# Four conditioned layers on one core: batch loops written out, one of eight scalings on GpSimd, v projected for two head pairs at once

## The chip, the core and the metric

The kernel runs on one core of one Trainium2 chip. The core has TensorE (matmuls, written PE in the profile, with its weight loads as PEld), VectorE (DVE), ScalarE (ACT), GpSimd (POOL) and SyncE (SP, which issues most DMAs). The metric is the device time of one execution in microseconds (us). Before the change it is 7090.01 us, the median of three runs (7084.36 to 7090.83).

## The reference

x is 8 x 512 x 256 in float32, and goes through four layers, each with a scale and shift from a condition vector:

- layers 0 and 2: attention with 16 heads of 16, then an MLP of 1024 ("narrow"; layer 2 has a padding mask and gates)
- layer 1: attention with 16 heads of 64, so q, k and v have 1024 columns each ("wide"), then an MLP
- layer 3: a selective state space layer (mamba) over the sequence in both directions, then a gated MLP

The parts that matter here, cut to the core:

```python
# layer 1
qkv = x @ W_qkv                      # 256 -> 3 * 1024
q, k, v = jnp.split(qkv, 3, axis=-1) # 16 heads of 64
attn = softmax(einsum('bqhd,bkhd->bhqk', q, k) * scale)
out = einsum('bhqk,bkhd->bqhd', attn, v)
...
# layer 3, one step of the scan, 512 channels (d) with 32 states (n) each
dA = jnp.exp(dt_t[:, :, None] * A)
hst = hst * dA + dt_t[:, :, None] * B_t[:, None, :] * x_t[:, :, None]
y = jnp.einsum('bdn,bn->bd', hst, C_t)
```

## The kernel before

x stays in SBUF for the whole kernel (`x_sb`). Each layer loads its weights, prepares the first batch row, and then runs a loop over the 8 batch rows: `with nc.Fori(0, B) as b` in the narrow layers (L659, used twice), the wide layer (L1082) and the mamba layer (L1723). Such a loop is one body of instructions with a branch back at its end and b in a register. An iteration is a block in which each engine has its own list of instructions, and semaphores order them between engines. It ends in a barrier of all engines, which also clears the semaphores; then come the loop's register operation and its compare-and-branch. The order on each engine is the order in which the Python code issues the instructions.

**Wide layer.** The 16 heads are 8 pairs; q, k and v of a pair fill 128 columns. `project(pair, which, to)` (L991) makes one of them, 512 columns of PSUM wide: for v it runs over 4 tiles of 128 tokens and 2 halves of the depth, with 128 columns of Wv moving, so 8 matmuls (16 records in the profile, since a float32 matmul leaves two). `projected` (L1004) copies the bank to SBUF on ScalarE. An iteration has 32 units (pair, tile of queries). Each has scores, maximum, exponential, a division on GpSimd (`normalise`, L1037), transposes, and the values of the pair before. Query, key and value of a pair (m = 0, 1, 2, ...) are projected in its first three units, two pairs ahead. TensorE heads the iteration, with the scores of a unit.

**Mamba layer.** 512 channels with 32 states are cut into 128 units per batch row: direction w, group g of two states, channel chunk c of 128, with c running fastest, so four units (IC = 4) share a group. For each unit:

- ScalarE makes `decay` = exp(dt * A) in two operations (`decay_unit`, L1803), three buffers deep
- ScalarE scales `dtx_T` (dt * x, tokens on partitions) by a column of B into `dtx_B` (`scale_pair`, L1791): 8 operations (OPS = 4 token tiles x 2 states) for a group of four units, two per unit, made six units ahead
- TensorE turns `dtx_B` around into PSUM (`fill_bx`, L1827) for unit i+1; ahead of a group's first unit it waits for all 8 scalings
- VectorE runs the scan over 2 x 512 elements (`scan_unit`, L1760)
- GpSimd multiplies the states by C, `hc` (L1751), four buffers deep
- TensorE adds `hc` up over the states in PSUM (`y_sum`, L1840), two units behind

At the start of the second direction VectorE also adds the first direction's sum to y, once behind each of four scans (`combine_first`, L1769). After the scans of a batch row comes a stretch called between, which ends this row (gate, output projection, MLP) and prepares the next.

Of the kernel before, what the change touches and what calls it, by code (L numbers as in the profile page):

```python
# [12 lines left out]
FP32 = mybir.dt.float32  # L13
# [7 lines left out]
P = 128  # L21
# [20 lines left out]
NJ = 2  # L42
# [312 lines left out]
def narrow_attention_layer(nc, consts, io, tag, mod0, eps, masked):  # L355
# [27 lines left out]
    with ExitStack() as ctx:  # L383
# [275 lines left out]
        with nc.Fori(0, B) as b:  # L659
# [258 lines left out]
def wide_attention_layer(nc, consts, io, tag, mod0, eps):  # L918
# [21 lines left out]
    with ExitStack() as ctx:  # L940
# [11 lines left out]
        v = sb("v", [P, RING, TT, P], FP32)  # L952
# [38 lines left out]
        def project(pair, which, to):  # L991
            cols = slice(pair * P, (pair + 1) * P)
            if which < 2:
                w = (wq, wk)[which]
                for c in range(DC):
                    last = nc.tensor.matmul(to, w[:, c, cols], hT[:, c, :], start=(c == 0), stop=(c == DC - 1))
            else:
                for t in range(TT):
                    for c in range(DC):
                        last = nc.tensor.matmul(to[:, t * P:(t + 1) * P], hT[:, c, t * P:(t + 1) * P], wv[:, c, cols],  # L1000
                                                start=(c == 0), stop=(c == DC - 1))
            last.then_inc(S["proj_filled"], 1)

        def projected(pair, which, of):  # L1004
# [4 lines left out]
            elif which == 1:  # L1009
                nc.scalar.activation(kT[:, pair % RING, :], of, ACT.Copy).then_inc(S["proj"], 1)  # L1010
            else:
                nc.scalar.activation(v[:, pair % RING, :, :].rearrange("p t n -> p (t n)"), of, ACT.Copy)\
                    .then_inc(S["proj"], 1)
# [68 lines left out]
        with nc.Fori(0, B) as b:  # L1082
# [4 lines left out]
            with nc.Block() as block:  # L1087
# [100 lines left out]
                def _(pe):  # L1188
# [11 lines left out]
                    def values(pair, k):  # L1200

                        if k == 0:
                            for j in range(2):
                                pe.wait_ge(S[f"probs_T{j}"], TT * (pair + 1))
                            if pair >= LEAD_PAIRS:
                                pe.wait_ge(S["proj"], 3 * (pair - LEAD_PAIRS + 1))
                            if pair:
                                pe.wait_ge(S["oT"], pair)
                        for j in range(2):
                            last = nc.tensor.matmul(bank[PV][head(j), :], v[:, pair % RING, k, head(j)],  # L1210
# [118 lines left out]
def mamba_layer(nc, consts, io, tag, mod0, eps):  # L1329
# [27 lines left out]
    with ExitStack() as ctx:  # L1357
        def sb(name, shape, dt, where=ctx):
# [23 lines left out]
            "y_init", "dtx", "dtxT_filled", "dtxT", "dt_rep", "zero", "c_rep", "dtxB", "decay", "bx_filled", "scan",  # L1382
# [340 lines left out]
        with nc.Fori(0, B) as b:  # L1723
            nxt = (b + 1) % B
            x_of_b = x[:, bass.ds(b, 1), :, :].rearrange("p b t d -> p (b t) d")
            with nc.Block() as block:
# [15 lines left out]
                def _(pool):  # L1742
                    nc.gpsimd.memset(decay[:, :, :, 0:1], 0.0).then_inc(S["zero"], 1)
                    for i in range(UNITS):
                        if i % IC == 0:
# [44 lines left out]
                def _(act):  # L1790
                    def scale_pair(q):  # L1791
# [5 lines left out]
                        for op in (2 * c, 2 * c + 1):  # L1797
# [28 lines left out]
                def _(pe):  # L1826
                    def fill_bx(i):  # L1827
                        k, c = i // IC, i % IC
                        if c == 0:
                            pe.wait_ge(S["dtxB"], OPS * (k + 1))  # L1830
# [136 lines left out]
```

## Time and profile before

| what | us |
|---|---|
| runs, median of 3 | 7090.01 (7084.36 to 7090.83) |
| the profiled execution | 7084.28 |
| its span, first to last instruction | 7082.4 |
| layer 0, with what comes first (12 to 1098) | 1086 |
| wide layer's loop (1098 to 2678) | 1580, TensorE busy 1509.27 |
| layer 2 (2678 to 3796) | 1118 |
| mamba layer's loop (3796 to 7068) | 3272, ScalarE busy 2881.24, VectorE 2771.48, TensorE 2698.68, GpSimd 2076.94 |
| busy over the span | PE 86%, PEld 45%, DVE 67%, ACT 64%, POOL 35% |

Times in the profile are microseconds from the start of the span, unless marked ns. A row of a timeline has start, length, engine, line, operation, out<-in and how many were merged (x4); in brackets stands how long the engine sat idle before it, and what ended that: "<-ACT l__decay L1808" is ScalarE's instruction of line 1808, a q behind an engine is its sequencer (waits, branches, barriers), and "issue" means that it waited for nothing that the profile shows. A row of a group has count, busy time, mean ns of one, and the idle time ahead of its instructions. Records of ScalarE overlap by about a tenth, so the pace of one is read from starts or counts, not from its length. The granted clock of TensorE (PEclk) is 1.00 at 2.4 GHz and 0.50 at 1.2 GHz; over the span it is 0.940.

### The profile page before, as it was taken

The page shows a single profiled execution, that of the slowest core. Times are in us where ns is not written, and L with a number is a line of the kernel's source. Part 1 is how long each engine was busy: PE and PEld are TensorE (multiplying, and loading weights), DVE is VectorE, ACT ScalarE, POOL GpSimd, SP SyncE. Part 2 cuts the span into 40 slices and gives each one's busy share as a digit, 9 for nine tenths or more (in the row PEclk, how much of TensorE's full clock was granted, in tenths as well). Part 3 has the DMA queues.
Part 4 walks back from the last instruction along what each step waited for, and adds up shares of the span by engine and source line. Part 5 has one row for each costly group of instructions (what it writes and reads, how often), then busy time and mean ns, then how long its engine had stood idle before and what let it go on. Part 6 is the DMA issues. An engine that isn't in the chain of part 4 may idle for free. (4 is left out here: it accounts for less than half of the span.)

```text
span 7082.4 us, 80931 instructions
## 1 busy us (share of the span) xinstructions
PE 6066.9 (86%) x29464; PEld 3179.4 (45%) x29464; DVE 4715.9 (67%) x5217; ACT 4502.5 (64%) x7301; POOL 2499.3 (35%) x1718
## 2 busy tenths in 40 slices
PE   6998988999999996898977878878888888888887
PEld 3544444555555553444443444444444444444444
DVE  4666654433433445666666979889797979979797
ACT  2343434544444452443437979798897979889796
POOL 0000002222222220000004838477483847658383
PEclk8999999999999997999998989999898989989898
DMA  3313140000000002313131010110101010010102
GB/s 104 54 27 54 27 83 8 1 1 1 1 1 1 1 1 51 57 29 57 29 72 43 28 38 27 27 37 20 46 27 37 28 36 29 19 48 26 39 27 56
DMA packets 162612, 229.57 MB, mean 32 GB/s; under 512 B 24784, under 2 KB 97816, under 8 KB 161776
## 3 DMA queue, kind: packets, MB, share of 16 engines
q1 hardware_dynamic: 162144, 225.09, 14.2%
q8 instruction: 215, 3.52, 0.2%
q14 instruction: 109, 0.89, 0.0%
q10 hardware_dynamic: 144, 0.07, 0.0%
HBM read 153.06 MB, written 33.72 MB: 26 GB/s over the span
## 5 line engine op out<-in xcount | busy, mean ns | idle before, releaser
L1766 DVE TENSOR_TENSOR_SCAN l__h<-l__decay,l__psum 128x1024 f32<-128x1024 f32 x1024 | 2331.9, 2284 | 208.2 <-ACT l__decay L1808 145.0
L1751 POOL TENSOR_TENSOR l__hc<-l__h,l__c_rep 128x1024 f32<-128x1024 f32 x1024 | 2050.5, 2002 | 545.1 <-DVE l__h L1766 509.3
L1835 PE MATMUL l__psum<-ident,l__dtx_B 128*128 128x128 f32 x8192 | 1141.4, 284 | 494.4 <-ACT l__dtx_B L1799 475.7
L1835 PEld LDWEIGHTS l__psum<-ident,l__dtx_B 128*128 128x128 f32 x8192 | 898.1, 143 | 1328.9 <-ACT l__dtx_B L1799 698.9
L1799 ACT ACTIVATE l__dtx_B<-l__dtx_T,l__b_T 128x512 f32<-128x512 f32 x2048 | 1353.2, 711 | 0.1
L1808 ACT ACTIVATE l__decay<-l__dt_rep,l__a_neg 128x511 f32<-128x511 f32 x2048 | 1351.5, 711 | 0.0
L1846 PE MATMUL l__psum<-l__hc,l__gather 128*64 128x512 f32 x4096 | 1108.6, 620 | 17.1 <-POOL l__hc L1751 17.1
L107 POOL TENSOR_SCALAR l__ln_var_eps<-l__ln_mean_var 128x4 f32<-128x4 f32 x70 | 16.0, 229 | 2447.6 <-DVE l__ln_mean_var L93 2447.6
L566 DVE TENSOR_REDUCE l__row_max<-l__psum 128x1 f32<-128x512 f32 x1072 | 688.4, 686 | 257.3 <-PE l__psum L581 255.8
L1039 POOL TENSOR_SCALAR l__probs<-l__probs,l__rec 128x512 f32<-128x512 f32 x516 | 352.4, 696 | 1013.0 <-DVE l__rec L1035 1013.0
L752 ACT ACTIVATE l__probs<-l__psum 128x1024 f32<-128x1024 f32 x512 | 515.6, 1025 | 272.4 <-PE l__psum L799 267.9
L1025 DVE TENSOR_REDUCE l__neg_max<-l__psum 128x2 f32<-128x1024 f32 x258 | 315.2, 1222 | 472.3 <-PE l__psum L1019 472.3
L581 PE MATMUL l__psum<-l__k_stack,l__q_stack 96*128 96x512 bf16 (+1 forms) x1072 | 435.1, 418 | 143.1 <-PEq L915 92.8
L1160 ACT ACTIVATE l__probs_T<-l__psum 128x512 f32<-128x512 f32 x256 | 152.8, 597 | 471.0 <-PE l__psum L1196 471.0
L1030 ACT ACTIVATE l__probs<-l__psum,l__neg_max 128x512 f32<-128x512 f32 x516 | 349.4, 683 | 47.3 <-DVE l__neg_max L1025 30.1
L1019 PE MATMUL l__psum<-l__kT,l__qT 64*128 64x512 f32 x1032 | 298.6, 656 | 62.7 <-issue 50.3
L799 PE MATMUL l__psum<-l__q_stack,l__k_stack 98*128 98x512 bf16 (+1 forms) x1024 | 330.3, 413 | 8.7 <-ACT l__probs L752 4.4
L1196 PEld LDWEIGHTS l__psum<-ident,l__probs 128*128 128x128 f32 x2048 | 224.8, 143 | 203.6 <-POOL l__probs L1039 121.7
L581 PEld LDWEIGHTS l__psum<-l__k_stack,l__q_stack 96*128 96x128 bf16 (+1 forms) x1072 | 103.2, 98 | 443.0 <-DVE l__row_max L566 294.0
L902 PE MATMUL l__psum<-l__w,l__g 128*128 128x256 f32 x1024 | 285.6, 380 | 12.4 <-ACT l__g L772 12.4
L1846 PEld LDWEIGHTS l__psum<-l__hc,l__gather 128*64 128x64 f32 x4096 | 203.8, 135 | 204.5 <-issue 130.0
L1196 PE MATMUL l__psum<-ident,l__probs 128*128 128x128 f32 x2048 | 288.6, 284 | 0.7
(168 smaller groups left out, 7112.9 us busy)
## 6 DMA issues: line engine op xcount, KB each, us to landing
l__c_rep<-l__c_dram SPq DMA_DIRECT2D x512, 128.0 KB, 2.8
l__dt_rep<-l__dt SPq DMA_DIRECT2D x144, 256.0 KB, 5.0
l__parts_dram<-l__parts SPq DMA_DIRECT2D x72, 384.0 KB, 4.5
l__q_stack<-l__parts_dram SPq DMA_DIRECT2D x216, 128.0 KB, 6.8
l__k_stack<-l__parts_dram SPq DMA_DIRECT2D x216, 128.0 KB, 9.8
l__w<-in_l_w SPq DMA_DIRECT2D x6, 1024.0 KB, 9.0
mod_w<-in_mod_w SPq DMA_DIRECT2D x2, 2816.0 KB, 12.6
x_sb<-in_x SPq DMA_DIRECT2D x1, 4096.0 KB, 27.3
```

The source lines that it names most:

```text
L566: nc.vector.tensor_reduce(mx[:, h // GH, t, h % GH:h % GH + 1], max_bank(n), AX.X, ALU.max).then_inc(S["max_taken"], 1)
L581: nc.tensor.matmul(max_bank(n), qs[0:k_max, h, t * P:(t + 1) * P], ks[0:k_max, h, :], start=True, stop=True).then_inc(S["max_filled"], 1)
L752: nc.scalar.activation(probs[:, n % SLOTS:n % SLOTS + 2, :], pair(n), ACT.Exp, scale=float(HD) ** -0.5).then_inc(S["exp"], 1)
L1030: nc.scalar.activation(probs[:, u % SLOTS, j, :], bank[QK + 2 * (u % 2) + j], ACT.Exp, bias=neg_max[:, u % SLOTS, j:j + 1], accum_out=sums ...
L1039: nc.gpsimd.tensor_scalar(probs[:, u % SLOTS, j, :], probs[:, u % SLOTS, j, :], rec[:, u % SLOTS, j:j + 1], 1.0, ALU.mult, ALU.mult)\
L1196: last = nc.tensor.transpose(bank[TR + j][:, k * P:(k + 1) * P], probs[:, u % SLOTS, j, k * P:(k + 1) * P], ident[:, :])
L1751: nc.gpsimd.tensor_tensor(hc[:, i % HCS, :, :], h[:, i % HS, :, :], c_of_i, ALU.mult).then_inc(S["hc"], 1)
L1766: nc.vector.tensor_tensor_scan(both(h[:, i % HS, :, :]), both(decay[:, i % DECAYS, :, :]), both(bx_psum(i)), 0.0, ALU.mult, ALU.add).then_ ...
L1799: nc.scalar.activation(dtx_B[:, k % 2, t, :, j, :], dtx_T[:, w, t, :].rearrange("p (b d) -> p b d", d=HB), ACT.Copy, scale=b_T[:, w, t, NJ ...
L1808: nc.scalar.activation(decay[:, i % DECAYS, s, 1:T], dt_rep[:, w, c, s, 1:T], ACT.Exp, scale=a_neg[:, g, c, s:s + 1]).then_inc(S["decay"], 1)
L1835: last = nc.tensor.transpose(bx_psum(i)[:, s, t * P:(t + 1) * P], dtx_B[:, k % 2, t, 2 * c + s, :, :].rearrange("p j d -> p (j d)"), ident ...
L1846: last = nc.tensor.matmul(y_psum[half(s), c, :], gather[:, :], hc[:, i % HCS, s, :], start=(g == 0), stop=(g == GROUPS - 1))
```

## The change

Three edits.

1. All three `nc.Fori` become Python loops: the body stands in the program eight times, b is a number, and there is no branch back. The barrier and the clearing of semaphores stay.
2. In the mamba layer the last of a group's 8 scalings (tile 3, state 1) goes from ScalarE to GpSimd, as a tensor_scalar with its own semaphore, `dtxB_pool`. GpSimd makes it one group ahead. TensorE's wait ahead of a group is now for 7 scalings of ScalarE per group and one of GpSimd.
3. In the wide layer a v projection covers 256 columns (two pairs) and two of the four token tiles; the two projections of two neighbouring pairs together make what they made before. The buffer of v is laid out for this: 2 slots of double width in place of 4. Values of an even pair wait for both.

```diff
-        with nc.Fori(0, B) as b:
+        for b in range(B):
...
-        v = sb("v", [P, RING, TT, P], FP32)
+        v = sb("v", [P, RING // 2, TT, 2 * P], FP32)
...
             else:
-                for t in range(TT):
+                both = slice(pair // 2 * 2 * P, (pair // 2 + 1) * 2 * P)
+                for u in range(2):
+                    t = pair % 2 * 2 + u
                     for c in range(DC):
-                        last = nc.tensor.matmul(to[:, t * P:(t + 1) * P], hT[:, c, t * P:(t + 1) * P], wv[:, c, cols],
-                                                start=(c == 0), stop=(c == DC - 1))
+                        last = nc.tensor.matmul(to[:, u * 2 * P:(u + 1) * 2 * P], hT[:, c, t * P:(t + 1) * P],
+                                                wv[:, c, both], start=(c == 0), stop=(c == DC - 1))
...
-                                pe.wait_ge(S["proj"], 3 * (pair - LEAD_PAIRS + 1))
+                                pe.wait_ge(S["proj"], 3 * (pair // 2 * 2 + 2 - LEAD_PAIRS))
...
                     nc.gpsimd.memset(decay[:, :, :, 0:1], 0.0).then_inc(S["zero"], 1)
+
+                    def scale_last(k):
+                        w, g, _ = split(k * IC)
+                        t, j = TT - 1, NJ - 1
+                        if k >= 2:
+                            pool.wait_ge(S["bx_filled"], IC * (k - 1))
+                        nc.gpsimd.tensor_scalar(dtx_B[:, k % 2, t, :, j, :],
+                                                dtx_T[:, w, t, :].rearrange("p (b d) -> p b d", d=HB),
+                                                b_T[:, w, t, NJ * g + j:NJ * g + j + 1], 1.0,
+                                                ALU.mult, ALU.mult).then_inc(S["dtxB_pool"], 1)
+
+                    scale_last(0)
                     for i in range(UNITS):
+                        if i % IC == 0 and i // IC + 1 < UNITS // IC:
+                            scale_last(i // IC + 1)
...
-                        for op in (2 * c, 2 * c + 1):
+                        for op in (2 * c, 2 * c + 1)[0:1 if c == IC - 1 else 2]:
...
-                            pe.wait_ge(S["dtxB"], OPS * (k + 1))
+                            pe.wait_ge(S["dtxB"], (OPS - 1) * (k + 1))
+                            pe.wait_ge(S["dtxB_pool"], k + 1)
```

ScalarE at the start of a batch row of the mamba layer, in the kernel before (L1799 is the scaling, L1808 the decay):

```order
226 L1799 ACT_TABLE_LOAD
227 L1799 ACTIVATE l__dtx_B<-l__dtx_T,l__b_T 128x8x64 x8
228 L1808 ACTIVATE l__decay<-l__dt_rep,l__a_neg 128x511 x4
229 L1799 ACTIVATE l__dtx_B<-l__dtx_T,l__b_T 128x8x64 x4
230 L1808 ACTIVATE l__decay<-l__dt_rep,l__a_neg 128x511 x2
231 L1799 ACTIVATE l__dtx_B<-l__dtx_T,l__b_T 128x8x64 x2
232 L1808 ACTIVATE l__decay<-l__dt_rep,l__a_neg 128x511 x2
233 L1799 ACTIVATE l__dtx_B<-l__dtx_T,l__b_T 128x8x64 x2
```

The same place after the change (L1816 is now the scaling, L1825 the decay):

```order
1251 L1816 ACTIVATE l__dtx_B<-l__dtx_T,l__b_T 128x8x64 x7
1252 L1825 ACT_TABLE_LOAD
1253 L1825 ACTIVATE l__decay<-l__dt_rep,l__a_neg 128x511 x4
1254 L1816 ACTIVATE l__dtx_B<-l__dtx_T,l__b_T 128x8x64 x4
1255 L1825 ACTIVATE l__decay<-l__dt_rep,l__a_neg 128x511 x2
1256 L1816 ACTIVATE l__dtx_B<-l__dtx_T,l__b_T 128x8x64 x2
1257 L1825 ACTIVATE l__decay<-l__dt_rep,l__a_neg 128x511 x2
1258 L1816 ACTIVATE l__dtx_B<-l__dtx_T,l__b_T 128x8x64
```

One scaling of the first eight is gone, and every fourth pair after them is a single one. The load of the function table, which stood ahead of the first scaling, now stands ahead of the first decay; it is one per batch row as before.

GpSimd at the same place, before:

```order
93 L1721 ISA
94 L1723 UNCONDITIONAL_BRANCH
95 L1741 UNCONDITIONAL_BRANCH
96 L1743 MEMSET l__decay 128x6
97 L1751 TENSOR_TENSOR l__hc<-l__h,l__c_rep 128x1024 x128
98 L107 TENSOR_SCALAR l__ln_var_eps<-l__ln_mean_var 128x4
```

And after:

```order
252 L1724 ISA
253 L1744 UNCONDITIONAL_BRANCH
254 L1746 MEMSET l__decay 128x6
255 L1753 TENSOR_SCALAR l__dtx_B<-l__dtx_T,l__b_T 128x8x64 x2
256 L1768 TENSOR_TENSOR l__hc<-l__h,l__c_rep 128x1024 x4
257 L1753 TENSOR_SCALAR l__dtx_B<-l__dtx_T,l__b_T 128x8x64
258 L1768 TENSOR_TENSOR l__hc<-l__h,l__c_rep 128x1024 x4
```

Two scalings now stand ahead of the first product, and one ahead of every fourth.

TensorE at a turn of the wide layer's loop, before (rows 179 and on are the body's head, to which the branch goes back):

```order
303 L1019 MATMUL l__psum<-l__kT,l__qT 128x512 x2
304 L1290 MATMUL l__psum<-l__w,l__g 128x256 x32
305 L1087 UNCONDITIONAL_BRANCH
306 L1082 REGISTER_ALU
307 L1082 COMPARE_AND_BRANCH
```

And the first turn after the change, with the first v projection (L1002):

```order
1315 L1293 MATMUL l__psum<-l__w,l__g 128x256 x32
1316 L1090 UNCONDITIONAL_BRANCH
1317 L1190 UNCONDITIONAL_BRANCH
1318 L1022 MATMUL l__psum<-l__kT,l__qT 128x512 x2
1319 L1199 MATMUL l__psum<-ident,l__probs 128x128 x8
...
1324 L1022 MATMUL l__psum<-l__kT,l__qT 128x512 x2
1325 L1199 MATMUL l__psum<-ident,l__probs 128x128 x8
1326 L1002 MATMUL l__psum<-l__wv,l__hT 128x256 x4
```

The register operation and the branch back are gone, the next row's scores follow at once, and a v projection has 4 matmuls of 256 columns where it had 8 of 128. The rest of the order on TensorE is the same.

## Rows read from the trace of the kernel before

**Rows 1.** Groups of instructions, mamba scans, 6700 to 6965 us; idle before them last:

```profile
L1766 DVE TENSOR_TENSOR_SCAN l__h<-l__decay,l__psum 128x1024 f32<-128x1024 f32 x109 | 248.7, 2285 | 16.3 <-ACT l__decay L1808 16.3
L1751 POOL TENSOR_TENSOR l__hc<-l__h,l__c_rep 128x1024 f32<-128x1024 f32 x109 | 218.2, 2002 | 48.8 <-DVE l__h L1766 48.0 <-PE l__psum L1846 0.8
L1799 ACT ACTIVATE l__dtx_B<-l__dtx_T,l__b_T 128x512 f32<-128x512 f32 x217 | 143.2, 706 | 0.0
L1808 ACT ACTIVATE l__decay<-l__dt_rep,l__a_neg 128x511 f32<-128x511 f32 x217 | 142.9, 705 | 0.0
```

**Rows 2.** Timeline of one group of four units: start, length, engine, line:

```profile
6703.79 2.29 DVE L1766 TENSOR_TENSOR_SCAN l__h<-l__decay,l__psum 128x1024 f32<-128x1024 f32 x1 [0.17 <-ACT l__decay L1808]
...
6706.22 2.00 POOL L1751 TENSOR_TENSOR l__hc<-l__h,l__c_rep 128x1024 f32<-128x1024 f32 x1 [0.45 <-DVE l__h L1766]
6706.24 2.29 DVE L1766 TENSOR_TENSOR_SCAN l__h<-l__decay,l__psum 128x1024 f32<-128x1024 f32 x1 [0.16 <-ACT l__decay L1808]
...
6707.43 1.09 PE L1835 MATMUL l__psum<-ident,l__dtx_B 128*128 128x128 f32 x8 [1.60 <-ACT l__dtx_B L1799]
```

**Rows 3.** Timeline of VectorE, second direction's start and scans at an iteration's end:

```profile
6829.05 2.27 DVE L1766 TENSOR_TENSOR_SCAN l__h<-l__decay,l__psum 128x1024 f32<-128x1024 f32 x1
...
6831.83 2.27 DVE L1766 TENSOR_TENSOR_SCAN l__h<-l__decay,l__psum 128x1024 f32<-128x1024 f32 x1
...
6973.25 8.82 DVE L1766 TENSOR_TENSOR_SCAN l__h<-l__decay,l__psum 128x1024 f32<-128x1024 f32 x4 [0.17 <-ACT l__decay L1808]
```

**Rows 4.** Timeline of GpSimd in the wide layer, a steady unit:

```profile
1309.97 1.36 POOL L1039 TENSOR_SCALAR l__probs<-l__probs,l__rec 128x512 f32<-128x512 f32 x2 [2.44 <-DVE l__rec L1035]
```

**Rows 5.** Timeline of a turn of the wide layer, VectorE's and TensorE's first:

```profile
1292.48 0.17 DVE L1101 COPY l__cur<-mod 128x12 f32 x1 [1.83 <-PEq L1296]
...
1295.95 2.08 PE L1019 MATMUL l__psum<-l__kT,l__qT 64*128 64x512 f32 x4 [7.48 <-issue]
```

**Rows 6.** Timeline of the entry into the wide layer's loop:

```profile
1098.09 2.08 PE L1019 MATMUL l__psum<-l__kT,l__qT 64*128 64x512 f32 x4 [6.12 <-PEq L1080]
1098.23 0.17 DVE L1101 COPY l__cur<-mod 128x12 f32 x1 [2.82 <-PEq L1080]
```

**Rows 7.** Instructions of line 1082: engine, count, ns min/median/max, first and last start:

```profile
L1082 PEldq COMPARE_BRANCH  x8: 79/3507/3849, 1292.0 to 2677.4; - x8
...
L1082 PEldq MOVE  x1: 29/29/29, 1098.0 to 1098.0; - x1
```

**Rows 8.** Timeline of mamba's loop: entry, first turn, last turn; GpSimd and ScalarE:

```profile
3796.40 0.11 POOL L1743 MEMSET l__decay<- 128x6 f32 x1 [78.35 <-POOLq L1721]
3796.41 1.28 ACT L1799 ACT_TABLE_LOAD   x1 [11.15 <-PEq L1721]
...
4203.34 0.11 POOL L1743 MEMSET l__decay<- 128x6 f32 x1 [51.32 <-POOLq L1860]
...
4205.96 1.28 ACT L1799 ACT_TABLE_LOAD   x1 [11.15 <-issue]
...
6658.99 0.11 POOL L1743 MEMSET l__decay<- 128x6 f32 x1 [50.99 <-POOLq L1860]
...
6661.89 1.28 ACT L1799 ACT_TABLE_LOAD   x1 [12.44 <-issue]
```

**Rows 9.** The same as rows 7, for line 659 of the narrow layers:

```profile
L659 PEldq COMPARE_BRANCH  x16: 76/211/242, 241.0 to 3700.9; - x16
```

**Rows 10.** Layer 0's first two rows: us, PE, PEld, DVE, ACT, POOL busy (count), PEclk:

```profile
125.80:241.20 115.40, 105.27 (x496) 52.75 (x496) 71.62 (x128) 49.44 (x59) 2.53 (x4) 0.96 0.26 42
241.20:356.70 115.50, 105.41 (x496) 52.92 (x496) 71.65 (x128) 49.47 (x59) 2.53 (x4) 0.96 0.27 41
```

**Rows 11.** Stretch at the first turn of the wide layer, columns as in rows 10:

```profile
1296.00:1300.60 4.60, 4.60 (x14) 2.58 (x15) 1.86 (x2) 1.49 (x4) 0.00 (x0) 0.50 0.03 7
```

**Rows 12.** Timeline of TensorE: a v projection, and a down projection:

```profile
1323.36 1.95 PE L1000 MATMUL l__psum<-l__wv,l__hT 128*128 128x128 f32 x16
...
1274.39 14.08 PE L1290 MATMUL l__psum<-l__w,l__g 128*128 128x256 f32 x64
```

More of the change, by code:

```diff
@@ L1011, in projected @@
             else:
-                nc.scalar.activation(v[:, pair % RING, :, :].rearrange("p t n -> p (t n)"), of, ACT.Copy)\
+                half = slice(pair % 2 * 2, pair % 2 * 2 + 2)
+                nc.scalar.activation(v[:, pair // 2 % 2, half, :].rearrange("p t n -> p (t n)"), of, ACT.Copy)\
                     .then_inc(S["proj"], 1)
@@ L1080, in wide_attention_layer @@
         nc.all_engine_barrier(sems_to_clear=S.range)
-        with nc.Fori(0, B) as b:
+        for b in range(B):
             nxt = (b + 1) % B
@@ L1209, in values @@
                         for j in range(2):
-                            last = nc.tensor.matmul(bank[PV][head(j), :], v[:, pair % RING, k, head(j)],
+                            last = nc.tensor.matmul(bank[PV][head(j), :], v[:, pair // 2 % 2, k, pair % 2 * P + HD1 * j:pair % 2 * P + HD1 * (j + 1)],
                                                     probs_T[:, pair % 2, j, k, :], start=(k == 0), stop=(k == TT - 1))
@@ L1381, in mamba_layer @@
             "dc_filled", "dc", "bT_filled", "bT", "c_out", "dt_filled", "abs", "exp_abs", "ln", "relu", "dt", "y_first",
-            "y_init", "dtx", "dtxT_filled", "dtxT", "dt_rep", "zero", "c_rep", "dtxB", "decay", "bx_filled", "scan",
+            "y_init", "dtx", "dtxT_filled", "dtxT", "dt_rep", "zero", "c_rep", "dtxB", "dtxB_pool", "decay", "bx_filled", "scan",
             "hc", "y_sum", "combine", "gated", "y_filled", "res", "up_filled", "silu", "prod", "down_filled"])
@@ L1721, in mamba_layer @@
         nc.all_engine_barrier(sems_to_clear=S.range)
-        with nc.Fori(0, B) as b:
+        for b in range(B):
             nxt = (b + 1) % B
```

## The prediction

> **What bounds the kernel now.** I read the page first (shares and the 40 slices in the table above), then the groups of instructions, then the timeline of single units and of the loops' turns, because the change touches three stages with different limits.
>
> The last layer's loop (mamba) takes 3272 of the 7082 us. In its scans the groups of one quiet stretch of 265 us [rows 1] show ScalarE with no idle time before any of its operations (0.0 in both groups, 217 + 217 operations). 265 / 434 gives 0.611 us for one, though each record is 0.71 long, because they overlap. VectorE's scan (2.285) waits 16.3 us there, all of it for ScalarE's decay; GpSimd's 109 products (2.002) wait 48.8 us, 0.45 each, for the scan. In the timeline [rows 2] a scan starts 0.16 us after VectorE came free, for a decay, and 2.45 us after the one before; in these ScalarE does two scalings and two decays, 0.6125 us each. TensorE waits 1.60 us once per group of four units, for the last dtx_B. So ScalarE sets this stage: 4 x 2.45 = 9.80 us per group, 256 groups in the kernel.
>
> What is next behind it? Where decays are ready, four scans take 8.82 us: (8.82 - 2.285) / 3 = 2.18 apart [rows 3]. That is 8.72 us a group. GpSimd has 4 x 2.00 = 8.0. TensorE has 9.80 - 1.60 = 8.2.
>
> In the wide layer TensorE is busy nearly all the time inside an iteration; at its turns it isn't, nor is anything else.
>
> **GpSimd scales one of eight.** ScalarE loses one operation per group, 32 per iteration, 256 in all: 256 x 0.6125 = 156.8 us. All of them lie ahead of the last scaling of an iteration, and only the last four scans are already at VectorE's pace [rows 3], so the whole sum reaches the end if 9.80 - 0.61 = 9.19 us per group can be held by the others:
> - VectorE needs 8.72. The decays now come 2.45, 2.45, 2.45 and 1.84 apart; after the short step a scan is 0.34 late, and the next two steps give it back. Where the second direction begins, a combination stands behind each of four scans, and they come 2.78 apart [rows 3]: 4 x 2.78 - 9.19 = 1.9 late, given back at 0.47 a group. ScalarE stalls only if scans are over 3.2 us late, so that is absorbed: its decays of unit i+2 start 1.4 us ahead of scan i+2, and wait for the end of scan i-1, which is the start of scan i, two scans of 2.3 earlier.
> - TensorE needs 8.2. Its first fill of a group waits for two semaphores; ScalarE's still comes last. That fill and the decay of the same unit end together now; the 0.34 above covers it. Behind the wait stand the y sums and three fills: they have 1.0 us left of the 1.6.
> - GpSimd gets the scaling: a tensor_scalar of 128x512 with a column as factor. The trace has this on GpSimd in the wide layer, two in 1.36 us [rows 4], one each 0.68. Sum 8.0 + 0.7 = 8.7 of 9.19. New is the form (8 pieces of 64, 128 apart in the destination). I bound it by 0.67 below and by the 2.00 of the two-input product above [rows 1], and take 0.68, the row with the same operation, inputs and size. The scaling is made a whole group ahead of its fill. It stands ahead of the product of the group's first unit, which then ends 0.6 us later; the y sum of it is behind a fill that waits for scan 4k+1, so nobody waits. Its wait for the buffer is met before it comes.
>
> **Loops written out: turns.** A turn has a barrier in both kernels; what goes is the branch back. In the wide layer TensorE starts 3.47 us after VectorE's first copy at a turn [rows 5], but 0.14 before it where the loop is entered without a branch [rows 6]. The sequencer's COMPARE_BRANCH lasts 3.51 us in the median against 0.03 for the MOVE at the entry [rows 7]; TensorE's scores head the iteration, so this is on the path: 7 x 3.5 = 24.6 us. In the mamba layer ScalarE heads the iteration. Its first instruction is 2.62 and 2.90 us behind GpSimd's memset at the first and the last turn, but 0.01 at the entry [rows 8]; with about 0.1 for the register work of the branch I take 2.8: 7 x 2.8 = 19.6 us. The table load that stood there now comes after the first seven scalings; there is still one, so the sum stays. In the narrow layers TensorE's branch takes 0.21 [rows 9]: 14 turns x 0.27 = 3.8 us.
>
> The Trainium skill has another price: by "Advanced Engine Details and Errata", section Control Flow Timing, a compare-and-branch costs about 108 ns. By it 28 turns would give 28 x 0.11 = 3 us in place of the 48. The narrow row is near it and the wide one 30 times above, so the rule doesn't hold for the long bodies; it is the third rival below.
>
> Does straight code run slower than a loop already passed? The narrow layer's first iteration runs code that no one has run before, the second repeats it: TensorE's 496 matmuls took 105.27 and 105.41 us in stretches of 115.4 and 115.5 [rows 10]. I cost it at nothing.
>
> TensorE's clock: after the turn it is granted 0.50 (1.2 GHz) for the wide layer's first 4.6 us [rows 11], behind 7.5 us of idle TensorE [rows 5]. With 4 us idle the low stretch may go or fall wholly behind the start: 4.6 us at half the clock costs 2.3, so 7 x 2.3 = 16 us either way. I take 0, as both ends are equally near.
>
> **v for two head pairs.** 66 projections, each 16 records of 128 columns before, (1.95 - 0.28) / 15 = 0.112 apart, and 8 of 256 now; these stand 14.08 / 64 = 0.218 apart in the down projection [rows 12]. 16 x 0.112 = 1.79 against 8 x 0.218 = 1.74: 3 us in all, at least 0 if TensorE waits elsewhere. Values of an even pair now wait for the projection of the next pair, three later; but the projection of query 9 is ahead of them in TensorE's order and had already waited for 9 copies where 6 are asked. No copy is added.
>
> **Sum.** 156.8 + 24.6 + 19.6 + 3.8 + 3.1 = 208 us, against the profiled execution: 7084.3 - 208 = 6876. That execution is at the low end of the three runs; their median is 5.7 above it. I forecast 6878.
>
> **The rivals.**
> - GpSimd becomes the bound. For: it is the closest new load, its form is new, and a product that waits starts 0.14 us after the scan's end [rows 2]. Against: [rows 4]. If the strided scaling takes twice as long, 1.36, and a product 2.05, a group is 9.56 in place of 9.19: 256 x 0.37 = 95 back, 6972. Chance 0.10.
> - The turns stay, since new code has to be brought in for every block. Against it stand the entries, which are also new code. 48 us don't come: 6925. Chance 0.08 (by the skill's rule above: 6877 + 45 = 6922).
> - Slower than before: GpSimd's scaling at 2.0, the row of the product, with each product paying such a wait, 0.15: 4 x 2.15 + 2.0 = 10.6 a group against 9.80, 256 x 0.8 = +205, less 51 of turns and v: 7084 + 154 = 7238. It decides from a group of 10.0 us, a scaling of 1.4 in that case. Chance 0.03.
> - VectorE becomes the bound at 2.18 plus the 0.16 of a wait at each scan [rows 2], 9.36 a group: 256 x 0.17 = 44 back, 6921. Against: such waits only arise when VectorE is early. Chance 0.06.
>
> **Numbers.** The forecast has 0.73. It spans 6850 (clock stretches gone, 16, and the turns at their longest, 10) to 6895. For 8 in 10 I reach to the cases at 6921 and 6925: 6850 to 6930. A change under 0.2% (14 us) can't be told from none here; faster by more 0.94, within 0.02, slower 0.04.
>
> **What would show it.** Right: scans 2.30 us apart in the mean in quiet stretches, ScalarE still with 0.0 idle ahead of dtx_B and decay, 1792 scalings on ScalarE and 256 on GpSimd near 0.7 us, GpSimd's idle ahead of the products down to about 0.1 a unit; no COMPARE_BRANCH at the turns, TensorE starting within 0.3 us of VectorE's first copy. A mamba iteration goes from 409.5 to about 387 us, a wide one from 197.9 to 194. Wrong: ScalarE waiting for scans, TensorE waiting for GpSimd at the first fill of a group, GpSimd without idle time, or gaps called "issue" at new places where code is brought in.

## The result, and the profile after

The changed kernel takes 6866.4 us in the median of 4 runs (6864.8 to 6877.0), the one before 7087.2 on the same chip (4 runs, 7083.2 to 7090.8). The ratio is 0.9692, with a 95% interval of 0.9675 to 0.9709: 3.1% faster. The forecast was 6878, in a range of 6850 to 6930. The profiled execution of after took 6865.4 us, with a span of 6863.6. Both spans, cut where VectorE ends the last addition of each layer:

| stretch | before | after | change | predicted |
|---|---|---|---|---|
| start and layer 0 (narrow) | 1045.9 | 1042.9 | -3.0 | -1.9 |
| wide layer | 1630.2 | 1583.7 | -46.5 | -27.7 |
| layer 2 (narrow) | 1023.5 | 1026.1 | +2.6 | -1.9 |
| mamba layer | 3367.6 | 3195.1 | -172.5 | -176.4 |
| sum | 7067.2 | 6847.8 | -219.4 | -208 |

The saving is 11 us larger than forecast. The wide layer gave 19 us more and layer 0 1; layer 2 and the mamba layer gave 4.5 and 4 less. So the total came nearer than the wide layer's term did, which is partly luck.

The groups of after in a quiet stretch of the mamba layer, 6500 to 6765 us (busy and mean ns, then idle time before), answer to [rows 1]:

```profile
L1783 DVE TENSOR_TENSOR_SCAN l__h<-l__decay,l__psum 128x1024 f32<-128x1024 f32 x115 | 256.0, 2272 | 6.3 <-ACT l__decay L1825 3.8
L1768 POOL TENSOR_TENSOR l__hc<-l__h,l__c_rep 128x1024 f32<-128x1024 f32 x116 | 231.2, 2005 | 17.2 <-DVE l__h L1783 13.3 <-PE l__psum L1864 0.3
L1825 ACT ACTIVATE l__decay<-l__dt_rep,l__a_neg 128x511 f32<-128x511 f32 x228 | 165.6, 846 | 0.3 <-DVE l__h L1783 0.3
L1816 ACT ACTIVATE l__dtx_B<-l__dtx_T,l__b_T 128x512 f32<-128x512 f32 x193 | 144.2, 846 | 0.0
...
L1753 POOL TENSOR_SCALAR l__dtx_B<-l__dtx_T,l__b_T 128x512 f32<-128x512 f32 x27 | 18.9, 699 | 0.0
```

There are 115 scans in 265 us, 2.30 apart where 109 were 2.43 apart by the same count. ScalarE still has no idle time to speak of, and GpSimd's before its products is down from 48.8 to 17.2 us. The scans that begin two neighbouring groups, against [rows 2]:

```profile
6199.38 9.04 DVE L1783 TENSOR_TENSOR_SCAN l__h<-l__decay,l__psum 128x1024 f32<-128x1024 f32 x4 [0.17 <-ACT l__decay L1825]
...
6208.59 4.46 DVE L1783 TENSOR_TENSOR_SCAN l__h<-l__decay,l__psum 128x1024 f32<-128x1024 f32 x2 [0.16 <-ACT l__decay L1825]
```

They are 9.21 us apart. The row merges its four scans, since it leaves out idle time of about 0.1 us. Taken one by one they start at 6199.38, 6201.59, 6203.76 and 6206.14. Two of the four still wait for a decay, 0.17 and 0.11 us, and start 2.45 and 2.38 behind the one before. The two behind ScalarE's single scaling find their decays made and start 2.21 and 2.17 behind, which is VectorE's own pace.

The turns. First the wide layer, VectorE's and TensorE's first instructions and a v projection, against [rows 5] and [rows 12]:

```profile
1286.21 0.17 DVE L1104 COPY l__cur<-mod 128x12 f32<-128x12 f32 x1 [1.25 <-PEq L1299]
1286.21 1.13 PE L1022 MATMUL l__psum<-l__kT,l__qT 64*128 64x512 f32 x4 [3.43 <-PEq L1299]
...
1295.81 1.89 PE L1002 MATMUL l__psum<-l__wv,l__hT 128*128 128x256 f32 x8
```

TensorE starts with VectorE, not 3.47 us behind it. It was idle for 3.43 us instead of 7.48, and the same four score matmuls take 1.13 us, not 2.08: they run at full clock. The v projection's eight records take 1.89 us where sixteen took 1.95. The stretches of 6 us behind the first, fifth and sixth turn show where that holds (length, busy time and count of PE, PEld, DVE, ACT and POOL, then the granted clock, DMA share and GB/s; compare [rows 11]):

```profile
1286.20:1292.20 6.00, 5.99 (x29) 3.25 (x30) 4.08 (x9) 3.08 (x7) 1.51 (x2) 1.00 0.00 0
...
2050.80:2056.80 6.00, 5.67 (x18) 2.85 (x20) 3.38 (x8) 2.12 (x6) 1.50 (x2) 0.72 0.01 3
2243.90:2249.90 6.00, 5.88 (x20) 2.92 (x20) 2.84 (x7) 2.38 (x6) 0.49 (x1) 0.72 0.01 3
```

At five of seven turns the clock stays at 1.00 (2.4 GHz), and the row behind them takes 191.17 us. At the fifth and sixth it is at 0.50 for part of the stretch, and the rows take 193.1 and 192.7. In the kernel before it was at 0.50 behind every turn.

The first turn of the mamba layer, against [rows 8]:

```profile
4135.64 0.11 POOL L1746 MEMSET l__decay<- 128x6 f32 x1 [51.09 <-POOLq L1878]
...
4135.66 4.40 ACT L1816 ACTIVATE l__dtx_B<-l__dtx_T,l__b_T 128x512 f32<-128x512 f32 x7 [8.02 <-PEq L1878]
...
4140.08 1.28 ACT L1825 ACT_TABLE_LOAD   x1
```

ScalarE starts 0.02 us behind GpSimd instead of 2.62; the table load stands behind the seven scalings. A mamba row takes 387.2 to 387.8 us (one 389.0) instead of 409.6 (one 408.3).

### The profile page after: what moved, and what is told of

The parts are those of the page before. It is cut to its first block and busy times, and to the rows that moved or that the text cites. A ratio compares the mean times of both kernels' runs of the same rounds, so it can differ in the third digit from the quotient of the medians.

```text
span 6863.6 us, 79140 instructions
## 1 busy us (share of the span) xinstructions
PE 6055.9 (88%) x28936; PEld 3147.6 (46%) x28936; DVE 4662.2 (68%) x5217; ACT 4353.0 (63%) x7044; POOL 2655.6 (39%) x1974
## 5 line engine op out<-in xcount | busy, mean ns | idle before, releaser
L1783 DVE TENSOR_TENSOR_SCAN l__h<-l__decay,l__psum 128x1024 f32<-128x1024 f32 x1024 | 2279.5, 2273 | 115.5 <-ACT l__decay L1825 92.4
L1825 ACT ACTIVATE l__decay<-l__dt_rep,l__a_neg 128x511 f32<-128x511 f32 x2048 | 1491.2, 850 | 2.4 <-DVE l__h L1783 2.3
L1816 ACT ACTIVATE l__dtx_B<-l__dtx_T,l__b_T 128x512 f32<-128x512 f32 x1792 | 1334.7, 845 | 69.6 <-PEq L1878 59.7
L581 PE MATMUL l__psum<-l__k_stack,l__q_stack 96*128 96x512 bf16 (+1 forms) x1072 | 436.4, 419 | 138.3 <-PEq L915 88.5
```

The lines of the kernel that those rows point to most:

```text
L581: nc.tensor.matmul(max_bank(n), qs[0:k_max, h, t * P:(t + 1) * P], ks[0:k_max, h, :], start=True, stop=True).then_inc(S["max_filled"], 1)
L1783: nc.vector.tensor_tensor_scan(both(h[:, i % HS, :, :]), both(decay[:, i % DECAYS, :, :]), both(bx_psum(i)), 0.0, ALU.mult, ALU.add).then_ ...
L1816: nc.scalar.activation(dtx_B[:, k % 2, t, :, j, :], dtx_T[:, w, t, :].rearrange("p (b d) -> p b d", d=HB), ACT.Copy, scale=b_T[:, w, t, NJ ...
L1825: nc.scalar.activation(decay[:, i % DECAYS, s, 1:T], dt_rep[:, w, c, s, 1:T], ACT.Exp, scale=a_neg[:, g, c, s:s + 1]).then_inc(S["decay"], 1)
```

## The experiments

The parts alone come first, all against runs of before on the same chip (median 7092.3).

**e1, the scaling alone.** The kernel before, with part 2 of the change and none of the others.

```diff
+                    scale_last(0)
...
-                        for op in (2 * c, 2 * c + 1):
+                        for op in (2 * c, 2 * c + 1)[0:1 if c == IC - 1 else 2]:
```

> The kernel before with one of a group's 8 scalings on GpSimd, loops and v as before. Theory (ScalarE sets the stage, 9.80 us per group becomes 9.20): 256 x 0.60 = 154 us less, 6931, and the mamba rows lose 19 us each, the first as the others; turns keep the 2.6 us of ScalarE behind GpSimd. Rival (part of the 172 us that the mamba layer lost comes from straight code or the clock, not from the scaling): under 140 us less, with groups above 9.3 us.

Measured: 6941.0 us, ratio 0.9793 (0.9777 to 0.9810), 151 less. The groups from 5000 to 5080 us:

```profile
L1780 DVE TENSOR_TENSOR_SCAN l__h<-l__decay,l__psum 128x1024 f32<-128x1024 f32 x36 | 80.4, 2274 | 2.3 <-ACT l__decay L1822 1.5
L1765 POOL TENSOR_TENSOR l__hc<-l__h,l__c_rep 128x1024 f32<-128x1024 f32 x36 | 71.7, 2001 | 5.2 <-DVE l__h L1780 4.0
L1822 ACT ACTIVATE l__decay<-l__dt_rep,l__a_neg 128x511 f32<-128x511 f32 x71 | 46.8, 707 | 0.0
L1813 ACT ACTIVATE l__dtx_B<-l__dtx_T,l__b_T 128x512 f32<-128x512 f32 x61 | 40.7, 708 | 0.0
```

ScalarE still never stops. The mamba layer takes 3214.2 us, 153.4 less, with groups of 9.18 to 9.19. This part of the mamba layer's gain doesn't need straight code. Layer 2, untouched here, took 1033.2 us instead of 1023.5; of that below.

**e2, the loops alone.**

```diff
-        with nc.Fori(0, B) as b:
+        for b in range(B):
```

(three times)

> The kernel before with all three loops written out and nothing else. Theory (a branch less at each turn, and TensorE's clock kept at the wide turns): wide turns 7 x (3.5 + 2.5) = 42, mamba turns 7 x 2.6 = 18, narrow layers 3 less in layer 0 and 3 more in layer 2, in all 60 us less, 7024. Rival 1 (the branch alone, as predicted): 48 less, 7036. Rival 2 (branches cost 0.11 us each): 3 less, 7081.

Measured: 7033.3 us, ratio 0.9923 (0.9906 to 0.9939), 59 less. The total is as my theory has it, its parts aren't. Wide rows are 194.5 us, 3.4 below 197.9, and not 191.9: the clock is still at 0.50 behind six of the seven turns, and for part of the stretch at the first (a row of 193.3). Mamba rows are 406.2, 3.4 less instead of 2.6. Layer 0 is 2.5 shorter, layer 2 is 1.2 shorter.

The 3.4 has two parts. TensorE started 4.8 to 5.3 us behind the last addition of the row before; now it starts 1.25 behind it (1.48 at one turn). That is 3.7 us in the mean. But the clock is low for 6.0 us behind that start where it was low for 5.3, which at half the clock takes 0.37 back. Take from each of the seven wide rows TensorE's start and half of the time at 0.50 behind it, and 190.26 to 190.27 us are left in the kernel before, 190.26 to 190.35 here.

**e3, the wide loop alone.** The same edit in the wide layer only.

> The kernel before with the wide layer's loop alone written out. Theory (branch 3.5 us a turn, and the stretch at 1.2 GHz behind it gone, which cost 2.3 to 2.5): wide rows from 197.9 to 191.9 us, some of them 1.7 longer where the clock still falls; 39 to 42 us less in all, 7043. Rival (the branch alone, the low stretch only moves): rows of 194.4, 25 less, 7060; the 46 us that the wide layer lost would then need v for the rest.

Measured: 7062.2 us, ratio 0.9962 (0.9947 to 0.9976), 30 less. Rows: 191.6, 193.6, then five of 194.45 to 194.55. Five are the rival's and one is the theory's: the rows get 3.4 shorter where the clock still falls, and keeping it comes on top only at some turns. In the whole layer 27.6 us are gone.

**e4, v for two pairs alone.**

> The kernel before with v projected for two pairs at once and nothing else. Theory: 66 projections, each 0.05 us shorter: 3 us less, 7081, not to be told from none by the time, but 0.4 us less in each wide row by the trace. Rival (256 columns are worth more in this place, or a wait on values goes): wide rows shorter by 1 to 2.5 us, 8 to 20 us in all, 7066 to 7076, which would explain the wide layer's surplus without the clock.

Measured: 7089.8 us, ratio 0.9997 (0.9987 to 1.0007), no difference by the time. By the trace the wide layer is 4.0 us shorter; with TensorE's start and the low clock taken out as above, all seven rows are 0.46 shorter (189.8 for 190.27). So v doesn't hold the wide layer's surplus by its own work.

**e5, TensorE late and idle.** The changed kernel; at seven turns TensorE first waits for GpSimd.

```diff
+    LATE = 5
...
+                    if b:
+                        for n in range(LATE):
+                            nc.gpsimd.tensor_scalar(g[:, n, :], hT[:, 0, :], 1.0, 1.0, ALU.mult,
+                                                    ALU.mult).then_inc(S["late"], 1)
...
+                    if b:
+                        pe.wait_ge(S["late"], LATE)
```

> The changed kernel, but at 7 turns of the wide layer TensorE waits for five scalings of 128x512 that GpSimd makes first (into a buffer that isn't in use there). Clock theory: TensorE starts 3.4 us later, as after the branch in the kernel before, its clock falls to 0.50 for the first 4 to 5 us, and a wide row gets 3.4 + 2.3 = 5.7 us longer: 35 to 40 us more than the changed kernel, 6903. Rival (the surplus of the wide layer has another cause than TensorE's idle time at the turn): 3.4 us a row, 24 more, 6890, clock at 1.00 behind the turn.

Measured: 6899.1 us, 33 above the changed kernel; the wide layer is 34 us longer. A turn of it in the timeline, and the 6 us behind VectorE's first copy:

```profile
1291.19 2.98 POOL L1097 TENSOR_SCALAR l__g<-l__hT 128x512 f32<-128x512 f32 x5 [12.87 <-SPq L1091]
1294.22 2.08 PE L1023 MATMUL l__psum<-l__kT,l__qT 64*128 64x512 f32 x4 [6.46 <-POOL l__g L1097]
```

```profile
1291.10:1297.10 6.00, 2.88 (x8) 1.38 (x9) 0.93 (x2) 0.00 (x0) 2.98 (x5) 0.50 0.00 0
```

TensorE is 3.0 us late (the five scalings stand 0.6 apart), idle for 6.46, and starts at 1.2 GHz at every turn: rows of 195.6 to 197.1, 4.5 to 5.9 above 191.17. The clock's part is 1.5 to 2.9 us a row. This run alters TensorE's idle time at the turn and none of its work: with 6.46 us in place of 3.43 the clock is at 0.50 at the start of seven rows out of seven, where it was at one.

**e6, TensorE late and busy.** The changed kernel with the first scores' matmuls six times more ahead of them.

```diff
+    MORE = 6
...
+                        for n in range(MORE):
+                            for j in range(2):
+                                nc.tensor.matmul(bank[QK + j], qT[head(j), 0, LEAD * P:(LEAD + 1) * P],
+                                                 kT[head(j), 0, :], start=True, stop=True)
```

> The changed kernel, but at 7 turns of the wide layer TensorE first makes the matmuls of its first scores six times more (the results are overwritten by the same). They take 6 x 0.57 = 3.4 us, the same delay as in the run with the wait. Clock theory: TensorE is busy, so the clock stays at 1.00 where it stood so before; 3.4 us a row, 24 more, 6890. Rival (a late start costs the 2.3 whatever TensorE does): 5.7 a row, 40 more, 6906.

Measured: 6911.3 us. I had mis-sized the matmuls. They appear as one row of the timeline at the first turn, and as one at the third:

```profile
1287.92 5.42 PE L1228 MATMUL l__psum<-l__kT,l__qT 64*128 64x512 f32 x24 [3.43 <-PEq L1305]
```

```profile
1682.23 7.12 PE L1228 MATMUL l__psum<-l__kT,l__qT 64*128 64x512 f32 x24 [3.42 <-PEq L1305]
```

At full clock they cost 5.2 us, and that row is 196.3 long, 5.1 above 191.17: a late start costs only its length if the clock stays. At the other six turns the clock was low for part of them, 1.7 us more, and rows are 198.0. So this run doesn't separate the theories by its total, and the clock theory's "stays at 1.00" did not come true. It shows something else: the idle time at the turn is 3.43 us as in the changed kernel, yet the clock falls at six turns where there it fell at two.

**e13, the idle time at the turn halved.** The loops alone (e2), and two matmuls at the end of a row.

```diff
+                    for n in range(2):
+                        nc.tensor.matmul(bank[TR], w1[:, n, 0:P], hT_mlp[:, n, :], start=(n == 0), stop=(n == 1))
```

> The kernel before with all loops written out, as in the run with the loops alone, and at the end of each wide row TensorE makes two matmuls more into a bank that nothing reads (1.9 us, while VectorE adds the last half of the row, so no later barrier). In the run with the loops alone TensorE's clock was at 0.50 for 5 us behind six of seven wide turns (rows of 194.5 us) and held at none but one (193.3). Theory (the clock falls for the 3.4 us that TensorE is idle at the turn): idle is 1.5 us now, the clock stays at 1.00, wide rows 191.6, 6 x 2.9 + 1.7 = 19 us less than 7033: 7014. Rival (idle time at the turn isn't what lets it fall): rows of 194.5 again, 7033.

Measured: 7016.9 us (7015.7 to 7021.3, 4 runs), ratio 0.9889 (0.9873 to 0.9906), 16 below the loops alone (on another chip). The start of a row in this run:

```profile
1287.67 1.13 PE L1019 MATMUL l__psum<-l__kT,l__qT 64*128 64x512 f32 x4 [1.71 <-PEq L1298]
```

Stretches behind the first three turns here, and then behind the same turns with the loops alone:

```profile
1287.60:1293.60 6.00, 5.93 (x18) 3.15 (x20) 3.38 (x8) 2.28 (x6) 1.50 (x2) 0.72 0.01 3
1480.90:1486.90 6.00, 5.92 (x29) 3.20 (x30) 4.01 (x9) 3.01 (x7) 1.50 (x2) 1.00 0.01 4
1672.60:1678.60 6.00, 6.00 (x29) 3.23 (x30) 4.09 (x9) 3.09 (x7) 1.51 (x2) 1.00 0.00 0
```

```profile
1287.00:1293.00 6.00, 5.93 (x18) 3.12 (x20) 3.38 (x8) 2.29 (x6) 1.51 (x2) 0.72 0.00 0
1480.30:1486.30 6.00, 5.93 (x15) 3.31 (x16) 2.89 (x7) 1.93 (x5) 0.54 (x1) 0.50 0.03 7
1674.90:1680.90 6.00, 5.98 (x15) 3.30 (x16) 2.94 (x7) 1.93 (x5) 0.59 (x1) 0.50 0.00 0
```

In 6 us TensorE makes 29 matmuls instead of 15. Rows are 191.63 at five of seven turns (193.3 and 193.5 at the other two), 2.9 below 194.5, with more work in them. The wide layer is 15.6 us shorter, and the clock's worth is measured: 2.9 us a turn.

The cause isn't shown by this run alone. The first turn has the same partial fall as with the loops alone, and the changed kernel holds the clock at five turns too, with the full 3.43 us of idle time. All traces together say this: behind 6.5 to 7.5 us of idle time the clock was at 0.50 when TensorE started, at 28 turns of 28 (before, e1, e4, e5); behind 3.4 to 3.7 us it fell at 33 turns of 63 (e2, e3, e6 to e10, e12 and the changed kernel); behind 1.7 to 1.9 us, at 2 of 7. So the long idle time brings the fall, which e5 shows by itself; at 3.4 us and below, idle time alone doesn't settle it.

**e12, the changed kernel again.** No edit.

> The changed kernel once more, unaltered, for its profile and time on the chip of these runs. Theory (whether TensorE's clock falls at a wide turn is not settled by the program; two kernels with the same wide layer had rows of 191.15 throughout and rows of 191.2 to 194.2): the wide rows again are 191.2 where the clock holds and 192.7 to 194.5 where it falls, but not in the same rows as in the first profile; mamba groups again 9.20. Rival (the program settles it): the same rows as in the first profile, 193.1 and 192.7 at the sixth and seventh.

Measured: 6869.4 us (6860.0 to 6871.6, 5 runs), ratio 0.9686 (0.9673 to 0.9699). The theory fell: wide rows are 191.17 with 193.08 and 192.71 at the sixth and seventh, as in the first profile, to 0.03 us. The pattern comes back in the same program. It isn't settled by the wide layer's own code, which is the same in e7, e8 and e10 below: there the clock falls behind none of the seven turns, five, and three. Mamba groups are 9.19.

**e10, narrow loops kept.** The changed kernel with `nc.Fori` in layers 0 and 2.

> The changed kernel with the loop of the narrow layers (0 and 2) kept as a loop. Theory (the branch costs 0.27 us a turn there, and the changed kernel's longer rows in layer 2 are the clock's, not the straight code's): layer 0 gets 2 to 3 us longer, layer 2 the same but for its clock, 3 to 4 us in all, under what the time can tell. Rival (straight code costs layer 2 time): layer 2 loses no rows of 120.1 us and the kernel is 3 to 6 us faster.

Measured: 6881.5 us (6859.1 to 6882.8, 5 runs), ratio 0.9696 (0.9680 to 0.9712), which overlaps that of e12 in the same comparison. The trace: the last seven rows of layer 0 take 806.3 us as in the kernel before, against 803.0 in the changed one, 3.3 for seven turns. Layer 2 takes 1035.1 us, not less than 1026.1: straight code isn't what made it longer. The wide layer is 6 us longer: 4 in its seven rows, through the clock at the first three turns, and 2 ahead of the end of its first row. The prediction has no term for what stands behind the end of a loop. Up to the end of the first row the wide layer takes 243.1 to 244.8 us in the five traces with narrow loops (before, e1, e3, e4, e10), 242.0 to 242.7 in the others.

Now the next bound behind ScalarE.

**e7, the scaling made twice.** The changed kernel; after GpSimd's scaling the same again, with a wait for the first.

```diff
+                        pool.wait_ge(S["dtxB_pool"], 2 * k + 1)
+                        nc.gpsimd.tensor_scalar(dtx_B[:, k % 2, t, :, j, :],
...
```

> The changed kernel with GpSimd's scaling made twice in a row into the same place. GpSimd then has 4 x 2.005 + 2 x 0.70 = 9.4 us of work per group, ScalarE 9.20 as before. Theory (GpSimd costs the group nothing until its own sum is above ScalarE's): 9.4 to 9.5 per group, 256 x 0.2 to 0.3 = 51 to 77 us more than the changed kernel, 6917 to 6943, with GpSimd without idle time. Rival 1 (GpSimd is already bound up with each scan, so its work adds in full): 256 x 0.70 = 179 more, 7045. Rival 2 (nothing waits for GpSimd within buffers): no change.

Measured: 6896.3 us, ratio 0.9727 (0.9711 to 0.9743), 30 above the changed kernel (the mamba layer of the profiled execution is 19 us longer). Groups are 9.30 us where GpSimd has come to bind, and still 9.19 in about the first ten of a row. In a stretch of eight groups (5126.30 to 5200.74 us) its products have no idle time before them, and VectorE now waits for them:

```profile
L1788 DVE TENSOR_TENSOR_SCAN l__h<-l__decay,l__psum 128x1024 f32<-128x1024 f32 x34 | 75.0, 2267 | 4.4 <-POOL l__hc L1773 3.4 <-ACT l__decay L1830 1.0
L1773 POOL TENSOR_TENSOR l__hc<-l__h,l__c_rep 128x1024 f32<-128x1024 f32 x33 | 65.1, 2003 | 0.0
```

A second scaling of 0.70 costs the group 0.11. The theory has the mechanism right and the size wrong: 30 us instead of 51 to 77, since GpSimd is faster than was taken, as the next run shows.

**e8, two of eight on GpSimd.**

```diff
+        on_pool = lambda k: 2
...
+                        for op in range(OPS - on_pool(k), OPS):
...
+                            if op >= OPS - on_pool(k):
+                                continue
```

> The changed kernel with two of a group's 8 scalings on GpSimd in place of one. ScalarE has 14 x 0.613 = 8.6 us per group, VectorE 8.72, GpSimd 4 x 2.005 + 2 x 0.70 = 9.4. Theory (GpSimd becomes the bound): 9.4 to 9.5 per group, 51 to 77 us more than the changed kernel, 6917 to 6943. Rival (ScalarE still is, or GpSimd runs beside it): 8.7 to 8.8 per group, 100 to 128 less, 6740 to 6766.

Measured: 6872.6 us, ratio 0.9690 (0.9674 to 0.9706), no different from the changed kernel. Neither expectation was right; the groups are 9.19. GpSimd in its timeline:

```profile
5150.89 1.41 POOL L1755 TENSOR_SCALAR l__dtx_B<-l__dtx_T,l__b_T 128x512 f32<-128x512 f32 x2
5152.21 7.92 POOL L1770 TENSOR_TENSOR l__hc<-l__h,l__c_rep 128x1024 f32<-128x1024 f32 x4
5160.07 1.41 POOL L1755 TENSOR_SCALAR l__dtx_B<-l__dtx_T,l__b_T 128x512 f32<-128x512 f32 x2
```

It never stops. Two scalings are followed by the products after 1.32 us and these by the next scalings after 7.86; that is 0.66 for a scaling and 1.965 for a product where the records say 0.70 and 2.0. 7.86 + 1.32 = 9.18, by chance the same as ScalarE's 15 x 0.613. In the changed kernel GpSimd has 7.86 + 0.66 = 8.5 of 9.19.

**e9, three of sixteen on GpSimd.** As e8, with this in place of its first line:

```diff
+        on_pool = lambda k: 1 + k % 2
```

> The changed kernel with GpSimd making one scaling of a group and two of the next in turn, 3 of 16. ScalarE then has 14.5 x 0.613 = 8.9 us per group, GpSimd, at 0.60 for one scaling as measured with two per group ((9.19 - 4 x 2.00) / 2), 8.0 + 1.5 x 0.60 = 8.9, VectorE 8.72. Theory (the stage goes at the longest of the three sums): 8.9 to 8.95 per group, 256 x 0.25 to 0.30 = 64 to 77 us less than the changed kernel, 6790 to 6803, the fastest so far. Rival (with no slack on any engine the waits between them add up, or the odd groups hold the even ones): 9.1 to 9.2, no gain, 6850 to 6875.

Measured: 6816.7 us (6805.6 to 6819.7, 5 runs), ratio 0.9611 (0.9598 to 0.9624), against 0.9686 (0.9673 to 0.9699) for the changed kernel in the same comparison: 53 us less, and 275 less than before. It is the fastest version, though short of the 64 to 77 us that were expected. Groups of a stretch of eight (5092.75 to 5163.01 us):

```profile
L1785 DVE TENSOR_TENSOR_SCAN l__h<-l__decay,l__psum 128x1024 f32<-128x1024 f32 x34 | 74.4, 2262 | 0.3 <-ACT l__decay L1829 0.3
L1770 POOL TENSOR_TENSOR l__hc<-l__h,l__c_rep 128x1024 f32<-128x1024 f32 x33 | 65.4, 2045 | 0.0
L1829 ACT ACTIVATE l__decay<-l__dt_rep,l__a_neg 128x511 f32<-128x511 f32 x64 | 42.0, 709 | 0.0
```

VectorE, GpSimd and ScalarE are all without idle time. Once VectorE has caught up, in the later groups of each direction, they are 9.05 and 8.71 in turn, 8.88 in the mean, as forecast; ahead of that they are 8.71, VectorE's pace; ScalarE has 14.5 x 0.613 = 8.89. The mamba layer gains 56.5 us and not 256 x 0.31 = 79. Of the 22 that are missing, ScalarE's idle time ahead of its decays is 10.7 us in the whole run, all of it waiting for scans: where the second direction begins, the combinations make scans late by more than its lead. The rest stands at the rows' ends: from the last scan's start to the row's end it is 88.5 to 89.3 us and 87.1 to 87.7 in e12, 1.6 more in the mean. That GpSimd's last products now come late is the likely cause; no run tests it.

## Why the prediction was right, point by point

The largest term, 157 of 208 us, rests on the right mechanism, and e1 shows it by itself. The nearness of the rest is partly luck: one term was taken as 0 and gave 15 us, others fell 8.5 short.

- **GpSimd's scaling, 156.8 us.** Right. Alone it gives 153.4 in the mamba layer. The steady group is 9.19, as worked out from [rows 2]; most of the 3 missing come at the start of a row's scans, where the first two groups take 9.05 and 8.88 us after 8.99 and 9.80 before, 0.9 less instead of 1.2.
- **GpSimd has room.** Right, and with more room than said: 0.66 for the scaling, where 0.68 was taken and 0.67 was the lower bound, but 1.965 for a product where 2.00 was read from records. Its limit is two scalings a group, where the predicted prices put it at (9.19 - 8.0) / 0.68 = 1.75. The rivals with a scaling of 1.36 or 2.0 are out.
- **VectorE absorbs the combinations.** Right for the changed kernel; ScalarE's idle time ahead of the decays is 2.4 us in the whole run. In e9, with less room, it is no longer absorbed in full, which takes back 10.7 us.
- **Wide turns, 24.6 us.** The branch: right. Without it TensorE starts 3.7 us earlier in the mean, 26.0 us over seven turns (predicted 3.5 and 24.6); with the low clock that follows, rows get 3.4 shorter in e2 and e3. What the Trainium skill gives for a compare-and-branch in "Advanced Engine Details and Errata", section Control Flow Timing, about 108 ns, is 30 times too low there.
- **TensorE's clock, taken as 0.** This is the step that failed: "I take 0, as both ends are equally near" [rows 11]. Behind TensorE's starts at the seven turns the clock was low for 36.9 us in the kernel before and is low for 6.6 in the changed one, which at half the clock is 15 us; the bound of 16 was the right end. By rows, where 194 was predicted: 197.9 before, 194.5 without the branch (e2), 191.63 with the clock held (e13), 191.17 with v as well. The sign couldn't have been read from [rows 5] and [rows 6]. They show a start at 1.2 GHz behind 7.48 and 6.12 us of idle time, and no row of before shows what 3.4 us do. With the loops alone the clock even took 1.3 us (39.6 us low behind the starts). So the range, which reached down by these 16 us, says what could be known, and the 0 in the sum doesn't.
- **The wide layer's surplus, 18.8 us.** 15.1 are the clock's and 1.4 the starts'. Of the rest most stands up to the end of the first row, which comes 2.7 us sooner. By e10, 2.2 us of that go with the narrow layers' loop; why it costs them behind its end was not traced.
- **v, 3.1 us.** Right: 4.0 in e4, and 0.46 a row (7 x 0.46 = 3.2) both there and between e13 and the changed kernel.
- **Mamba turns, 19.6 us.** Mis-sized: 3.4 a row in six of seven by e2 where 2.8 was taken. The layer is 24 us shorter there, 22 in the seven rows. ScalarE's start gave 2.6 and GpSimd's, which now comes 1.21 us behind VectorE's last addition and came 1.54 behind it, 0.3. The remaining 0.5 is at the row's end: from the last scan's start it takes 87.3 us in the mean before and 86.8 in e2, where the clock is low for 27 us of it instead of 31. The parts alone give the mamba layer 153.4 + 24.2 = 178 us and the changed kernel 172.5. Of the 5 between them 3 are lost up to the end of the first row; their cause stays open.
- **Narrow turns, 3.8 us.** Half right. Layer 0's seven rows lose 3.3 us (1.9 predicted). In layer 2 no gain is seen: rows of 116.6, 118.3 and 120.1 us, the last with the clock at 0.93 in the mean and the others at 0.95. Before they took 117.1 and 118.5.
- **Straight code is not slower.** Right; no long idle time called "issue" at new places (TensorE's before the first scores of a row, 50 us in all, is gone), and e10, with the narrow loops back, is not faster.
- **The parts and the whole.** 151 + 59 + 3 = 213 against 223 for the changed kernel on the same chip (7092.1 - 6869.4). The wide layer has 27.0 + 4.0 = 31 in the parts and 46.5 together: v doesn't gain it, but with all edits the clock happens to hold at five turns, and with the loops alone at none of the seven fully. Why at these turns, for the same idle time of 3.4 us, stays open: no run tests it. It comes back with the same program (e12) and differs between programs with the same wide layer (e7, e8, e10), so it isn't a property of the edit, and another edit elsewhere may take it away.

## What to carry to other kernels

Ask of every gap that a change shortens on TensorE what the clock was granted behind it, and price both cases: here 3.4 us a turn where the clock still fell, and 2.9 on top where it held. Put the second into the range until a run shows which it is, and not as a mean into the sum. Price the next bound by start-to-start distances in a row that has no waits, not by the length of records: the room on GpSimd was two scalings, not 1.75, and splitting 3 of 16 between the engines gave another 53 us. Add up parts by their stages, not by the total, since a layer that nobody touched can move by 10 us.

## What the runs showed of the hardware

- A layer's time depends on the clock that it meets. Layer 2, with the same loop code, took 1023.5 us in before, 1033.2 in e1, 1033.1 in e4 and 1035.1 in e10; with straight code 1022.2 to 1034.4 (e2, e6). The granted clock is 0.92 in the mean in before and e2, 0.91 in the four others. This is as large as several of the terms in question.
- Without the branch at the end of a long body a row is 3.4 us shorter in the wide and the mamba layer; in layer 0, with its short body, 0.5 (3.3 / 7).
- Time at the low level costs half of itself in a row that TensorE fills: with TensorE's start and half of the low time behind it taken out, the 14 wide rows of before and e1 agree to 0.02 us (190.26 to 190.28), although the low time behind the start runs from 4.1 to 5.6 us.
- In the first profile of after ScalarE's scalings and decays have records of 0.85 us in the mean, in its second and in all others 0.71, at the same distance of 0.61 from one to the next. The length of a record that overlaps with the next is no price.
- By the Trainium skill's "TensorE: Matmul & The Clock Gate", section "What's actually happening", the throttled state is the default and activity releases it. The runs agree: idle for 6.9 to 7.5 us (before) and 6.5 (e5), TensorE starts at 0.50 at all seven turns.
